# A preparation stage merged into the attention that follows it

## What is computed

```python
xn = layernorm(x, ln_x_g, ln_x_b)            # x here: the context, 4 x 2048 x 512
ln = layernorm(latents, ln_l_g, ln_l_b)      # the normalised state, 4 x 128 x 512
q = (ln @ Wq).reshape(b, m, h, d)            # 16 heads of 64
kv = jnp.concatenate([xn @ Wkv, ln @ Wkv], axis=1)     # 2048 + 128 rows
qn = rmsnorm(q, qn_g) * scale
kn = rmsnorm(k, kn_g)
sim = jnp.einsum('bhid,bhjd->bhij', qn, kn)
attn = jax.nn.softmax(sim, axis=-1)
out = jnp.einsum('bhij,bhjd->bhid', attn, v)
out @ Wout + bout
```

## Time and profile before

| | |
|---|---|
| time, median of 3 runs (lowest to highest) | 2524.99 us (2524.52 to 2530.7) |
| profiled execution: time, span in the trace | 2526.58 us, 2524.8 us |
| PE busy | 2280.6 us, 90% of the span |
| DVE, ACT, POOL busy | 72%, 62%, 46% |
| DMA | 124 GB/s in the mean |
| granted PE clock, mean | 0.954 |

### The profile page before, as it was taken

The page is one execution under the profiler, slowest core; times in us unless marked ns, Lnnn a source line. Parts: engine busy times, 40 slices in busy tenths (PEclk is TensorE's granted clock), DMA queues, the critical chain, the costliest instruction groups (busy, mean ns, idle before and its releaser), DMA issues. The chain is left out here.

```text
span 2524.8 us, 57411 instructions
## 1 busy us (share of the span) xinstructions
PE 2280.6 (90%) x21754; PEld 1493.9 (59%) x22035; DVE 1827.6 (72%) x3374; ACT 1569.3 (62%) x2921; POOL 1149.7 (46%) x904
## 2 busy tenths in 40 slices
PE   5799999999999999998888699995899899998796
PEld 3346665666566656665446477773567676676442
DVE  7478777887778867777354599995777777767336
ACT  4347666666666666665334399993377677788423
POOL 4436676667666664555100000003367676656510
PEclk8899999999999999998899799997999999999797
DMA  6223333224322321124321599984443443334102
GB/s 211 51 73 89 87 104 86 79 74 120 85 75 77 104 78 42 39 56 158 111 98 51 180 367 362 361 331 168 152 134 120 128 122 112 98 91 142 66 1 86
DMA packets 256275, 313.58 MB, mean 124 GB/s; under 512 B 71792, under 2 KB 183024, under 8 KB 255104
## 3 DMA queue, kind: packets, MB, share of 16 engines
q1 hardware_dynamic: 252048, 301.76, 37.3%
q10 hardware_dynamic: 3312, 6.03, 0.6%
q0 software_dynamic: 640, 2.10, 0.3%
HBM read 226.23 MB, written 47.91 MB: 109 GB/s over the span
## 5 line engine op out<-in xcount | busy, mean ns | idle before, releaser
L816 POOL TENSOR_TENSOR a_plo<-a_p,a_phi 128x512 bf16<-128x512 f32 x272 | 321.5, 1182 | 357.2 <-ACT a_phi L870 356.5
L1075 PE MATMUL ps<-w,a_xhi 128*128 128x512 bf16 x1085 | 412.0, 380 | 6.5 <-PEq L3083 6.4
L1074 PE MATMUL ps<-w,a_xhi 128*128 128x512 bf16 x1085 | 411.7, 379 | 6.2
L1076 PE MATMUL ps<-w,a_xlo 128*128 128x512 bf16 x1073 | 407.3, 380 | 0.2
L2234 POOL TENSOR_TENSOR a_plo<-a_p,a_phi 128x512 bf16<-128x512 f32 x256 | 307.4, 1201 | 177.2 <-ACT a_phi L2271 168.4
L838 ACT ACTIVATE a_kraw<-ps 128x256 f32<-128x256 f32 x272 | 104.5, 384 | 371.8 <-PE ps L1076 370.1
L2366 DVE CUSTOM_DVE_ANT_0 a_junk<-ps,a_biasrow 128x512 bf16<-128x512 f32 x256 | 176.0, 688 | 115.1 <-PE ps L2506 91.5
L893 DVE TENSOR_TENSOR a_v<-ps,a_v 128x256 bf16<-128x256 f32 x272 | 114.3, 420 | 167.9 <-ACT a_v L840 166.9
L2266 ACT ACTIVATE a_p<-ps,a_mcol 128x512 f32<-128x512 f32 x256 | 175.0, 684 | 86.5 <-PE ps L2524 78.8
L781 POOL TENSOR_TENSOR a_rn<-a_rn,a_power 128x16 f32<-128x16 f32 (+1 forms) x80 | 204.0, 2550 | 6.7
L907 DVE SCALAR_TENSOR_TENSOR a_kraw<-a_kraw,a_rn 128x1024 f32<-128x1024 f32 (+1 forms) x80 | 149.3, 1866 | 78.3 <-POOL a_rn L781 78.3
(11 more groups left out here) (483 smaller groups left out, 6841.6 us busy)
## 6 DMA issues: line engine op xcount, KB each, us to landing
e_wst<-in_L_ffn_W SPq DMA_DIRECT2D x46, 2048.0 KB, 11.2
a_ks<-a_khi SPq DMA_DIRECT2D x256, 64.0 KB, 2.0
a_ks<-a_klo SPq DMA_DIRECT2D x256, 64.0 KB, 2.1
a_ct<-in_ctxT SPq DMA_DIRECT2D x16, 1024.0 KB, 6.3
a_ks<-k1h_d SPq DMA_DIRECT2D x128, 128.0 KB, 2.5
xa<-in_ctx SPq DMA_DIRECT2D x8, 1024.0 KB, 5.6
k1h_d<-a_khi SPq DMA_DIRECT2D x64, 128.0 KB, 2.0
k1l_d<-a_klo SPq DMA_DIRECT2D x64, 128.0 KB, 1.7
```

The source lines that it names most:

```text
L816: pool.tensor_tensor(p_lo[:, m % 3, :], p32[:, m % 2, :], p_hi[:, m % 3, :], ALU.subtract)\
L1074: pe.matmul(out, x_hi[:, c, tile], w_hi[:, c, g, :], start=(c == 0), stop=False)
L1075: pe.matmul(out, x_hi[:, c, tile], w_lo[:, c, g, :], start=False, stop=False)
L1076: last = pe.matmul(out, x_lo[:, c, tile], w_hi[:, c, g, :], start=False, stop=(c == C - 1))
```

## The change

The two stages become one, `cross0`. Before the steps begin, only the first part of batch 0's context and the first group of `Wkv` are prepared. The other three parts, the turned state and the other weight groups are prepared within steps 0 to 19, and each piece of that work stands at a step chosen by hand. The splitting of the weights moves from DVE and POOL to ACT (high part) and to DVE and POOL with one half each (low part); the roots of the norms are on POOL. The queries are no longer made all at once: those of unit 0 are made in steps 3 to 7 (`query_product(0)`, `query_turn`), and those of unit u+1 at place 12 of unit u, as one float32 product of 256 columns that goes into bank KT. Their norm and turn go with the last, short group of keys (`size` 2 instead of 1), and they reach `q_both` and `q_low` straight from SBUF. The weights of the query product are loaded one unit ahead (`wqs`), the float32 states of a batch come back from DRAM (`lq`). The second buffer for the context, `xn1`, is gone, and the tables of the context's normalisation are moved. Staging tiles lie in parts of `ks`, the ring of values and `kraw` that aren't used yet.

```diff
-    size = [4, 4, 4, 4, 1]
+    Q_MADE = 12
+    def size(u, j):
+        return 4 if j < 4 else 2 if u < UNITS - 1 else 1
...
-                    k_max[e + 5 + h].append((u, j, h))
+                    k_max[12 + 2 * j + h // 2 if u == 0 and j < 2 else e + 5 + h].append((u, j, h))
...
+            begin = at + ((10, 9, 6, 5)[j] if b == 1 else 5)
             for i in range(4):
-                ln_stat[at + ((9, 10, 13, 13) if late else (1, 2, 5, 5))[i]].append((b, j, i))
-                ln_norm[at + ((18, 21, 21, 22) if late else (10, 13, 13, 14))[i]].append((b, j, i))
-                ln_turn[at + ((25, 26, 29, 30) if late else (16, 17, 21, 22))[i]].append((b, j, i))
-            ln_rstd[at + (17 if late else 9)].append((b, j))
+                ln_stat[begin + (2, 3, 3, 4)[i]].append((b, j, i))
+                ln_norm[begin + (5, 5, 6, 6)[i]].append((b, j, i))
+                ln_turn[at + (((17, 21, 22, 25), (16, 17, 21, 22))[j] if b == 1 and j < 2 else (13, 16, 17, 21))[i]]\
+                    .append((b, j, i))
+            ln_rstd[begin + 4].append((b, j))
+            ln_load[begin].append((b, j))
...
+            def query_product(u):
+                if u == 0:
+                    pe.wait_ge(lt_done, C)
+                else:
+                    pe.wait_ge(lq_in, 16 * (u // QUADS + 1))
+                    bank_free(before_q[u])
+                pe.wait_ge(wq_in, 16 * (u + 1))
+                out = ps[:, KT if u else PV, 0:256]
+                for c in range(C):
+                    last = pe.matmul(out, lq[:, c, :] if u else LT[:, c, 0:P], wqs[:, c, :], start=(c == 0), stop=(c == C - 1))
+                last.then_inc(q_mm, 1)
...
+            for x in range(C):
+                head_turn(x)
             for n in range(FIRST, LAST):
                 m = n - LAG - VLAG
                 if 0 <= n < N:
                     project(n)
+                if n in (0, 1, 4, 5, 8, 9):
+                    x = 4 * (n // 4 + 1) + 2 * (n % 4)
+                    head_turn(x)
+                    head_turn(x + 1)
+                if n == 1:
+                    states_turn()
+                if n == 3:
+                    query_product(0)
+                if n == 6:
+                    query_turn()
                 for u, j, pr in k_turn[n]:
                     turn(u, j, pr)
                 for b, j, c in ln_turn[n]:
                     context(b, j, c)
+                u = unit_at(n, Q_MADE)
+                if u is not None:
+                    query_product(u + 1)
...
+                if n in (2, 5):
+                    head_stat(2 if n == 2 else 3)
+                if n in (3, 7):
+                    head_norm(2 if n == 3 else 3)
+                if n == 4:
+                    dve.wait_ge(q_cp, 1)
+                    dve.tensor_reduce(ms[:, 20:24], heads(q0_sq, DH0), AX.X, ALU.add).then_inc(q0_ss, 1)
+                if n == 5:
+                    dve.wait_ge(q0_root, 1)
+                    dve.scalar_tensor_tensor(heads(q0_raw, DH0), heads(q0_raw, DH0), DH0 ** 0.5,
+                                             per_head(rn[:, 20:24], 4, DH0), ALU.mult, ALU.mult).then_inc(q0_norm, 1)
...
+                if n in (10, 14, 19):
+                    weight_low({10: 1, 14: 2, 19: 3}[n])
...
-                stage(cross0_prepare, X, keep)
-                stage(cross0_attend, X, keep)
+                stage(cross0, X, keep)
```

More of the change, by code:

```diff
@@ L126, in cross0_prepare @@
[L126 to L147, removed]
@@ L590, in part, with unit_at @@
         return 16 * (b - 1) + 4 * j + c
-    before_turn, before_ln = {}, {}
+    def unit_at(n, place):
+        u, s = divmod(n, NT0)
+        return u if s == place and u < UNITS - 1 else None
+    before_turn, before_ln, before_q = {}, {}, {}
     held_by = None
@@ L600, in cross0_attend @@
             held_by = ("ln", part(*use) + 1)
-    def xn(n):
-        return (X, xn1)[n % 2]
+        if unit_at(n, Q_MADE) is not None:
+            before_q[unit_at(n, Q_MADE) + 1] = held_by
+            held_by = ("query", unit_at(n, Q_MADE) + 2)
     def bank_p(n):
@@ new lines, in head_load, with weights @@
+            def head_load(j):
+                sp.dma_start(head_context(j)[:], t["ctx"][0, j * 512:(j + 1) * 512, :].rearrange("(i p) d -> p i d", p=P))\
+                  .then_inc(c_in[j], 16)
+            def weights(g):
+                wkv = t["L0_xattn_Wkv"].rearrange("(c p) n -> p c n", p=P)
+                if g == 1:
+                    sp.wait_ge(l_tp, C)
+                if g >= 2:
+                    sp.wait_ge(w_lo_done[g - 2 if g == 2 else 2], 2)
+                for half in range(2):
+                    sp.dma_start(weight_stage(g)[:, :, half * 256:half * 256 + 256],
+                                 wkv[:, :, half * INNER + g * 256:half * INNER + g * 256 + 256])\
+                      .then_inc(w_in[g == 1], 16)
@@ new lines, in _ @@
+            for dst, src in ((gx, "L0_xattn_ln_x_g_col"), (bx, "L0_xattn_ln_x_b_col"),
+                             (gl, "L0_xattn_ln_l_g_col"), (bl, "L0_xattn_ln_l_b_col")):
+                sp.dma_start(dst[:], t[src]).then_inc(vec_in, 16)
+            weights(0)
+            head_load(1)
+            query_weights(0)
+            for dst, src in ((gq, t["L0_xattn_qn_g"]), (gk, t["L0_xattn_kn_g"])):
+                for h in range(2):
+                    sp.dma_start(dst[h * DH0:h * DH0 + DH0, :], src.rearrange("(d a) -> d a", a=1))\
+                      .then_inc(gv_in, 16)
@@ L730, in _ @@
+            head_load(2)
+            sp.dma_start(mcol8[:], t["mask0_col"]).then_inc(mcol_in, 16)
             mask_row(0)
-            sp.wait_ge(zero_done, 2)
-            queries(0)
-            queries(1)
+            sp.wait_ge(c_tp, C)
+            head_load(3)
+            weights(2)
             for n in range(LAST):
-                if n % NT0 == 7 and 2 <= n // NT0 + 1 < UNITS:
-                    queries(n // NT0 + 1)
+                if n == 3:
+                    weights(1)
+                    states_out()
+                if n == 4:
+                    query_weights(1)
+                    sp.wait_ge(l_out, 16)
+                    query_states(0)
+                if n == 6:
+                    sp.wait_ge(c_tp, 3 * C)
+                if n == 7:
+                    sp.wait_ge(zero_done, 2)
+                    queries(0, xs_hi[:, 0, 0:2 * P], xs_lo[:, 0, 0:2 * P])
+                if n == 9:
+                    states_parts_out()
+                    sp.wait_ge(lt_out, 32)
+                    latents(0)
+                if n == 16:
+                    weights(3)
+                if n == 22:
+                    for g in (1, 2, 3):
+                        sp.wait_ge(w_lo_done[g], 2)
+                u = unit_at(n, Q_MADE + 2)
+                if u is not None and u < UNITS - 2:
+                    query_weights(u + 2)
+                    if (u + 2) % QUADS == 0:
+                        query_states((u + 2) // QUADS)
@@ L737, in _ @@
                 for u, j, pr in k_turn[n]:
                     stack(u, j, pr)
+                    if j == 4 and u < UNITS - 1:
+                        x = turn_index(u, 4, 0) % KR
+                        queries(u + 1, k_hi[:, x, 2 * P:4 * P], k_lo[:, x, 2 * P:4 * P])
                 for b, j, c in ln_turn[n - 1] if n else []:
                     store(b, j, c)
+                for b, j in ln_load[n]:
+                    load(b, j)
                 for b in range(1, B):
```

656 lines of the change are left out of this document (314 added, 342 removed).

## The result

The changed kernel takes 2557.04 us (median of 4 runs, 2556.68 to 2564.66), the kernel before 2527.68 (4 runs, 2524.52 to 2530.7): ratio 1.0132, 95% interval 1.0111 to 1.0153. It is slower by 1.3%, where 2515 was forecast. The profiled execution took 2556.68 us, its span is 2554.8; 30.0 us more than before.

A forecast was written before the change was run, and what follows sets the result against it. PE was taken as full behind 174.7 us, with 44 us idle ahead of it. Terms -37.2 (head), +25.8 (added matmul work) and +1.5 (bank) summed to -9.9, giving 2515 us; range 2499 to 2533.

The forecast's parts named there:

- The head: Preparation and steps 0 to 24: first projection at 23.2 us, first maximum at 137.5 instead of 174.66, -37.2 us.
- steps 6, 11 and 17: Three PE stalls before the first maximum, about 5 us each, each followed by 1.8 us for the lower clock.
- The product: Query product of 256 columns priced by columns at 1.72 us; fourteen behind the first maximum add 24.1 us.
- rival 4: Query product costs up to 3.2 us as weight loads no longer hide; +21 in all, 2536 us; chance 0.06.
- two transposes: Last key group's two turns each have one tile more, the query: 28 x 0.108 = 3.0 us added.
- The bank: Product's result read with the short key group: chain 1.1 us later against 0.8 slack; 1.5 us taken in all.
- rival 2: Bank makes the turn behind the product wait in every unit: +5 to +14, 2519 to 2528 us; chance 0.20.
- three context turns that come earlier: Three turns of the next batch's context fall ahead of the first maximum, taking 1.3 us from the stretch behind it.
- context's single buffer: 1 MB context load lands before its first statistics: costs nothing, or at worst 2 us in 12 places.
- DMA stands at 28%: In the attention, loads of query weights and context have a whole unit as cover, so no cost was added.
- Rival 3: DVE blocked beside POOL in steps 0 to 24: +20 if all falls on the path, 2535 us; chance 0.09.

The follow-up runs named there:

- experiment 6: Changed kernel with three of the four row chunks of the query products of units 1 to 15 left out; 2548.13 us, ratio 1.0091.
- experiment 3: Changed kernel with the root and scaling of the short key group, with the query, one step later; 2550.24 us, ratio 1.0101.
- experiment 8: Kernel before with the context's load moved to place 5 and its statistics to places 7 to 9; 2552.33 us, ratio 1.0104.
- 10: Kernel before with only the context's statistics moved to places 7 to 9; 2541.83 us, ratio 1.0084.
- experiment 11: Kernel before with only the context's load moved two places ahead, to place 5, in front of the two key stacks; 2536.30 us, ratio 1.0057.
- experiment 5: Changed kernel with the splitting of weight group 1 two steps later, on ACT and in both low halves; 2551.96 us, ratio 1.0130.
- experiment 4: Changed kernel with the turn of unit 0's query, its high and low part and its stacking two steps later; 2561.59 us, ratio 1.0132.

## Why the prediction was wrong

*The head: the mechanism right, 4.5 us short.* First projection 24.7 (23.2 said), PE's waits at steps 6, 11 and 17 of 6.4, 5.1 and 5.2 us (5 each said), on the three releasers named, each with the lower clock behind it (12 us at 0.50, so some 6 us, where 3 x 1.8 was said); first maximum 142.0 (137.5, 4 either way, so half a us outside). -32.7 instead of -37.2. Of the 4.5 us the first projection brings 1.5; the rest isn't sized.

*The product: right.* 1.73 us against 1.72; experiment 6 took three quarters of it away and a late unit lost 1.30 of 1.29. The dear product (rival 4) is out. 14 x 1.94 for product and two transposes gives 27.2, the +27.1 of the sum.

*The bank: the mechanism right, the size off.* I had 0.8 us of slack and a chain 1.1 us longer, and took 1.5 us in all; rival 2 had 0.35 to 1 us a unit. The late units waited 0.64 each, units 3, 7 and 11 2.2, where POOL's mask delays the root: 8.6 us of waits where the kernel before had 3.9, and by experiment 3 11.4 us between the first and the last maximum (0.83 in a late unit). This term was mis-sized by 10 us.

*The failed step: the moved context.* Of the moved tables the prediction priced the three context turns that come earlier, -1.3. The load and the first statistics came up only under the context's single buffer, at "nothing, or at worst 2 us in 12 places, in the idle time of DVE"; and of all loads it said that "DMA stands at 28%". That is an upper bound of 24 us, and it went into neither the sum nor the range nor a rival. By experiment 8 the new places cost 28 us in the kernel before, without product or single buffer; by 10 and 11 the statistics alone cost 20 and the load alone 12. Two things were missed. DVE is not idle where the statistics went: at the start of a unit it makes the maximum, the seed and the old unit's result, and PE waits for each. And a DMA share of 28% says nothing of a queue: one load of 1 MB ahead of a 64 KB stack makes it land in 5.6 us instead of 2.0, two in the middle of a unit make PE wait 2.6 to 3.5, with a lower clock behind the wait in two of three cases. The one alone costs nothing where no context is read back (67.2 us in experiment 11). I followed the load to its own reader and not past the stacks that it overtakes in SP's order.

*Rival 3, DVE blocked by POOL,* forecast the right side for another reason. Its place was the head, where the first maximum is 4.5 us later than walked, not 20.

The sum with the measured terms: -32.7 head, +27.2 product and transposes, +11.4 bank, about +29 places, which is +35 up to the last of the maxima, where the profile has +35.5; with the 5.5 us less behind it, +30.0. So of the 40 us between this and the forecast of -9.9 the places are 29, the bank 10 and the head 4.5, and the 5.5 went the other way; some 2 us are left over.

## What to carry to other kernels

Where a full engine meets small transfers with a deadline, a moved large load is priced by what it overtakes in its queue, not by the mean share of the DMA engines. (No run here issues the load from another queue, so it isn't shown whether the order in the queue or the DMA engines that both share hold the stack up.) Where work is moved within a stage that is 98% full, look for the few places where the full engine waits for the moved work's engine, here the change from one unit to the next, and put the work anywhere else. An upper bound that was written down belongs into the range.

## What the hardware showed unexpectedly

- The halves of a weight group are in line with blocking, not sharing. POOL's half takes 2.12 or 2.13 us whether DVE's stands beside it or not. DVE's takes 1.22 us behind POOL's (experiment 5). Where it begins while POOL's runs, it ends 1.08 and 1.09 us after POOL's end (17.02 and 84.01): it takes 2.69 us when it begins 1.61 ahead of that end, and 2.09 when 1.00. So from POOL's start to DVE's end these two groups took 3.2 us; twice DVE's 1.22, an estimate for the whole group on DVE alone, is 2.4. In groups 2 and 3 the halves hardly meet, and DVE's takes 1.33 and 1.22. Timeline of the changed kernel, group 0 and group 1, then experiment 5, group 1:

```profile
14.90 2.12 POOL L608 TENSOR_TENSOR w<-a_ks,w 128x1024 bf16<-128x1024 f32 x1 [4.34 <-ACT w L756]
15.41 2.69 DVE L923 TENSOR_TENSOR w<-a_ks,w 128x1024 bf16<-128x1024 f32 x1
...
81.89 2.12 POOL L608 TENSOR_TENSOR w<-a_v,w 128x1024 bf16<-128x1024 f32 x1 [0.65 <-ACT w L756]
...
83.01 2.09 DVE L923 TENSOR_TENSOR w<-a_v,w 128x1024 bf16<-128x1024 f32 x1
```

```profile
85.37 1.22 DVE L923 TENSOR_TENSOR w<-a_v,w 128x1024 bf16<-128x1024 f32 x1
```

- Where loads and stacks share a queue, the same instructions in the same places took 76.2 or 80.3 us a unit in two executions (experiment 4): 2 us of it are idle PE, the other 2 a lower granted clock behind the waits, 0.94 instead of 0.98.
